# A gathered two-layer adapter with LayerNorm on one core: a new order of the first transfers, other runs of W1, two-part tables and later stores

## The reference

```python
w1 = W1[language_ids]                       # [512, 128] of ten
w2 = W2[language_ids]                       # [128, 512] of ten
h = relu(einsum('bsh,bha->bsa', hidden, w1) + b1[ids])
y = hidden + einsum('bsa,bah->bsh', h, w2) + b2[ids]
normed = (y - mean(y)) * rsqrt(var(y) + 1e-5)
out = x + normed * gamma[ids] + beta[ids]
```

## Time and profile before

| | us |
|---|---|
| median of 3 runs (316.99 to 318.69) | 318.01 |
| the profiled execution | 316.75 |
| its span | 315.0 |
| outside the span (316.75 - 315.0) | 1.75 |

### The profile page before, as it was taken

How to read it: one execution, slowest core, us unless ns; L and a number is a source line. 1 busy time by engine, 2 the same in 40 slices (tenths; PEclk the granted TensorE clock), 3 DMA queues, 4 the chain that set the end, 5 groups by cost and what they waited for, 6 DMA issues and landing times.

```text
span 315.0 us, 7506 instructions
## 1 busy us (share of the span) xinstructions
PE 289.5 (92%) x2008; PEld 253.8 (81%) x2039; DVE 289.8 (92%) x621; ACT 263.0 (83%) x601; POOL 186.2 (59%) x217
## 2 busy tenths in 40 slices
PE   1757959999999999999999999999999999999972
PEld 1237758889998888998888998888999888999861
DVE  5998856999999999999999999999999999999996
ACT  3977438889988889899989988999989988988872
POOL 2960742666655666565566665656656566665562
PEclk9968779999999999999999999999999999999998
DMA  5999999899999999899898989999898889885324
GB/s 155 332 389 372 293 331 390 276 340 352 358 347 328 321 313 302 302 318 318 292 315 313 299 309 310 318 302 311 290 319 311 315 304 311 286 291 202 116 110 177
DMA packets 56441, 94.03 MB, mean 298 GB/s; under 512 B 3387, under 2 KB 14711, under 8 KB 56273
## 3 DMA queue, kind: packets, MB, share of 16 engines
q1 hardware_dynamic: 56302, 93.41, 87.4%
q10 hardware_dynamic: 99, 0.14, 0.1%
HBM read 44.78 MB, written 33.55 MB: 249 GB/s over the span
## 4 chain that ended last, share of the span: by engine, by line
PE 79%; SPq 10%; issue 3%; DMA 3%; DVE 2%; DVEq 1%; ACT 0%
PE ps_h L504 33%; PE ps_y L525 28%; PE ps_T L488 16%; SPq L287 5%; DMA x_io<-in_x 2%; PE ps_h L497 2%; SPq L269 2%; SPq L257 1%; SPq L282 1%; DVE ps_y L663 1%; DVE ps_y L644 1%; SPq L172 1%; SPq L250 1%; DVEq L172 1%; DMA ids_raw<-in_itok_B 1%
## 5 line engine op out<-in xcount | busy, mean ns | idle before, releaser
L358 POOL TENSOR_TENSOR x_io<-x_io,beta_all 128x512 f32<-128x512 f32 x128 | 163.0, 1284 | 37.3 <-DVE ps_y L644 27.9
L504 PE MATMUL ps_h<-x_T,w_stage 128*128 128x128 f32 x1024 | 126.2, 277 | 0.0
L504 PEld LDWEIGHTS ps_h<-x_T,w_stage 128*128 128x128 f32 x1024 | 121.0, 194 | 0.8
L421 ACT ACTIVATE cut<-ps_y,row_sum 128x512 bf16<-128x512 f32 x128 | 87.9, 687 | 16.3 <-PE ps_y L525 11.4
L676 DVE SCALAR_TENSOR_TENSOR x_io<-ps_y,rstd,x_io 128x512 f32<-128x512 f32 x128 | 90.2, 747 | 2.6 <-DVE rstd L668 0.3
L663 DVE SCALAR_TENSOR_TENSOR ps_y<-ps_y,neg_mean,gamma_all 128x512 f32<-128x512 f32 x128 | 90.3, 750 | 1.7 <-ACT cut L421 1.7
L488 PE MATMUL ps_T<-identity,x_io 128*128 128x128 f32 x512 | 69.4, 280 | 11.2 <-DMA x_io<-in_x 10.1
L488 PEld LDWEIGHTS ps_T<-identity,x_io 128*128 128x128 f32 x512 | 62.2, 145 | 20.8 <-issue 12.6
L401 ACT COPY x_T<-ps_T 128x1024 f32<-128x1024 f32 x64 | 63.5, 992 | 6.7 <-PE ps_T L488 6.5
L525 PE MATMUL ps_y<-w_high,h_high 128*128 x128 | 62.3, 486 | 3.9 <-DVE w_low L625 2.2
L644 DVE SCALAR_TENSOR_TENSOR ps_y<-x_io,b_all 128x512 f32<-128x512 f32 x93 | 62.9, 704 | 0.0
(11 more groups left out here) (67 smaller groups left out, 150.9 us busy)
## 6 DMA issues: line engine op xcount, KB each, us to landing
x_io<-in_x SPq DMA_DIRECT2D x64, 512.0 KB, 5.1
out<-x_io SPq DMA_DIRECT2D x63, 512.0 KB, 3.9
w_stage<-w_all SPq DMA_DIRECT2D x58, 256.0 KB, 3.3
w_stage<-in_L_cond_W SPq DMA_DIRECT2D x12, 256.0 KB, 6.5
x_io<-in_L_cond_W SPq DMA_DIRECT2D x5, 512.0 KB, 7.8
b_all<-in_L_cond_b SPq DMA_DIRECT2D x1, 2560.0 KB, 14.3
w_all<-in_L_cond_W SPq DMA_DIRECT2D x5, 512.0 KB, 7.2
out<-x_io SPq DMA_DIRECT2D x2, 256.0 KB, 2.0
```

The source lines that it names most:

```text
L358: nc.gpsimd.tensor_tensor(x_slot(t), x_slot(t), of_lang(beta_all, lang), ALU.add).then_inc(x_beta_ready, 1)
L421: nc.scalar.activation(squares[:, t % 2, :], ps_y[t % Y_BANKS][:, :], ACT.Square, scale=-float(H), bias=stat(row_sum, t), accum_out=stat(s ...
L504: last = nc.tensor.matmul(bank[:, b * S:(b + 1) * S], w1_stage[:, 2 * (p % STAGE_PAIRS) + b, c, :], x_T[:, (2 * p + b) % 4, c, :], start=F ...
```

## The change

Seven things, none of which changes what is computed (gamma and beta are carried in two parts of float32r instead of three of bf16).

- SP's order: W2 chunks 0 and 1 ahead of the wait for the ids, then W1 of pair 0 and the other W2 chunks, then x and W1 of pairs 1 to 3 and x of pair 4; only then `b2_all`, and `w1_all` chunk by chunk between later loads.
- W1 of the first nine pairs comes from HBM, and a partition takes four neighbouring rows of it, one run of 2 KB instead of four of 512 B. So that the product is the same, the transposes of these nine pairs read every fourth column of x (`rows_of`).
- 24 slots of x. The store of a pair stands two turns later on SP, and a load waits for a store two turns old.
- gamma and beta are cut in two parts; TensorE's operand `signed_pick` (+1, -1) takes the difference. Their rows lie in `b2_all`, the parts in `w2_low`, until these are filled; hence four waits before `b2_all`.
- b1 is cut on GpSimd; b2 is centred on VectorE (`centre_b2`); the `pick` copy on ScalarE is gone.
- `put_b2` is gone: VectorE seeds the first four batches with x (`seed_x`), and TensorE adds b2 in S(0) and S(1).
- TensorE, ScalarE and VectorE take the beginning in another order; `copy_w1` is one step later.

```diff
-STAGE_HBM = 6
+STAGE_HBM = 9
+STORE_LAG = 2
@@ sync
+            load_x(0)
+            load_w2(0)
+            load_w2(1)
             sp.wait_ge(ids_ready, 1)
             stage_w1(0)
...
+            for p in range(1, 4):
+                load_x(p)
+                stage_w1(p)
+            load_x(4)
+            sp.wait_ge(b1_parts_ready, 1)
+            sp.wait_ge(b2_parts_ready, 1)
+            sp.wait_ge(beta_parts_ready, 1)
+            sp.wait_ge(gamma_parts_ready, 1)
             sp.dma_start(b2_all[:, :, :], b2.partition_broadcast(128)).then_inc(s_b2, 16)
...
-            for p in range(PAIRS - 1):
+            for p in range(PAIRS - 1 + STORE_LAG):
                 if p + STAGE_AHEAD < PAIRS:
                     stage_w1(p + STAGE_AHEAD)
-                sp.wait_ge(out_ready, 2 * p + 2)
-                sp.dma_start(out_pairs[:, p, :, :], x_pair_slots(p)).then_inc(stored[p % X_PAIRS], 16)
-                if p >= 1 and p - 1 + X_PAIRS < PAIRS:
-                    sp.wait_ge(stored[(p - 1) % X_PAIRS], x_loads(p - 1))
-                    load_x(p - 1 + X_PAIRS)
+                if p == 0:
+                    load_w1(4)
+                ahead = p + X_FIRST + 1
+                if ahead < X_PAIRS:
+                    load_x_behind_w2(ahead)
+                elif ahead < PAIRS:
+                    sp.wait_ge(stored[ahead % X_PAIRS], x_loads(ahead - X_PAIRS))
+                    load_x(ahead)
+                if p >= STORE_LAG:
+                    store(p - STORE_LAG)
@@ scalar
-            act.wait_ge(pick_step, 3)
-            nc.scalar.copy(pick[:, :, :], pick_row[:, :].unsqueeze(2).broadcast_to([128, L, 128])).then_inc(pick_ready, 1)
-            act.wait_ge(s_b2_rows, 16)
-            nc.scalar.activation(b2_cut[:, 1, :], b2_rows[:, :], ACT.Identity, accum_out=b2_sum[:, :])\
...
@@ tensor
+                rows_of = "s (p c) -> s c p" if t // 2 < STAGE_HBM else "s (c p) -> s c p"
+                columns = x_slot(t).rearrange(rows_of, c=C)
                 for c in range(C):
-                    last = nc.tensor.transpose(ps_T[:, t % 2, c, :], x_io[:, t % SLOTS, c * 128:(c + 1) * 128],
-                                               identity[:, :])
+                    last = nc.tensor.transpose(ps_T[:, t % 2, c, :], columns[:, c, :], identity[:, :])
...
-                table = parts[:, 0:H] if n < L else parts[:, H:2 * H]
-                nc.tensor.matmul(spread_bank(n), pick[:, n % L, :], table, start=True, stop=True).then_inc(spread, 1)
+                nc.tensor.matmul(spread_bank(n), signed_pick[:, n % L:n % L + 1].broadcast_to([128, 128]),
+                                 table_parts[:, n // L, :], start=True, stop=True).then_inc(spread, 1)
...
+            for p in range(FIRST):
+                first_half(p)
...
+            for p in range(FIRST, PAIRS):
+                n = p - FIRST
+                for b in range(2):
+                    second_product(2 * n + b, langs[n][b])
+                first_half(p)
```

More of the change, by code:

```diff
@@ L67, in build @@
         b2_all = sb("b2_all", [128, L, H], F32)
[L71 to L75, removed]
+        squares = sb("squares", [128, 2, H], BF16)
+        b2_parts = sb("b2_parts", [128, H], BF16)
+        table_parts = w2_low[:, L - 2:L, :]
+        rounded = b2_all[0:2 * L, 0:2, :].bitcast(F32R)
+        gamma_rows = b2_all[0:2 * L, 2, :]
+        beta_rows = b2_all[0:2 * L, 3, :]
+        b1_rows = b2_all[0:3 * L, 4, 0:A]
+        b2_rows = b2_all[0:3 * L, 5, :]
+        b2_cut = squares[0:3 * L, 0, :]
+        b1_cut = squares[0:3 * L, 1, 0:A]
         b1_parts = sb("b1_parts", [128, A], BF16)
@@ L187, in vector_seeds @@
             return t + 1 - scalar_seeds(t)
[L189 to L194, removed]
         def w1_stagings(q):
-            return sum(16 if scalar_copies(r) else 32 for r in range(q % STAGE_PAIRS, q + 1, STAGE_PAIRS))
+            return sum(32 if r < STAGE_HBM else 16 for r in range(q % STAGE_PAIRS, q + 1, STAGE_PAIRS))
         def wait_seed(engine, t):
@@ L266, in stage_w1, with load_w1 @@
                     sp.wait_ge(s_w1, 16 * W_CHUNKS)
-                table = w1_rows if q < STAGE_HBM else w1_all
-                for b in range(1 if scalar_copies(q) else 2):
+                table = w1_runs if q < STAGE_HBM else w1_all
+                for b in range(2 if q < STAGE_HBM else 1):
                     sp.dma_start(w1_stage[:, 2 * (q % STAGE_PAIRS) + b, :, :], table[:, bass.ds(langs[b], 1), :, :])\
                         .then_inc(w1_staged[q % STAGE_PAIRS], 16)
+            def load_w1(n):
+                langs = slice(n * LC, (n + 1) * LC)
+                sp.dma_start(w1_all[:, langs, :, :], w1_rows[:, langs, :, :]).then_inc(s_w1, 16)
@@ L272, in _, with load_x_behind_w2, store @@
+            def load_x_behind_w2(p):
+                sp.wait_ge(w2_low_ready, (p - X_FIRST + 1) * LC)
+                load_x(p)
+            def store(p):
+                sp.wait_ge(out_ready, 2 * p + 2)
+                sp.dma_start(out_pairs[:, p, :, :], x_pair_slots(p)).then_inc(stored[p % X_PAIRS], 16)
+            load_x(0)
+            load_w2(0)
+            load_w2(1)
             sp.wait_ge(ids_ready, 1)
             stage_w1(0)
-            load_w2(0)
-            load_w2(1)
-            load_x(1)
@@ L551, in _ @@
             pe.wait_ge(spread_dve, len(by_dve))
[L552 to L570, removed]
+            for p in range(FIRST):
+                first_half(p)
+            pe.wait_ge(ids_ready, 1)
+            langs = {p: langs_of(pe, p) for p in range(FIRST)}
+            pe.wait_ge(b2_parts_ready, 1)
+            pe.wait_ge(w2_low_ready, L)
+            for p in range(FIRST, PAIRS):
[3 more added lines that the diff above has]
+                first_half(p)
+                langs[p] = langs_of(pe, p)
             for n in range(PAIRS - FIRST, PAIRS):
@@ L585, in _ @@
             nc.vector.tensor_scalar(lang_ids[:, :], ids_fix[:, 1, :], 0.0, float(L - 1), ALU.max, ALU.min).then_inc(ids_ready, 1)
-            def cut_in_three(table, rounded, to, first, ready):
-                for k in range(2):
-                    nc.vector.tensor_copy(rounded, table).then_inc(cut_step, 1)
-                    dve.wait_ge(cut_step, first + 2 * k + 1)
-                    nc.vector.scalar_tensor_tensor(table, rounded, later_part[0:3 * L, k:k + 1], table,
-                                                   ALU.mult, ALU.subtract).then_inc(cut_step, 1)
-                    dve.wait_ge(cut_step, first + 2 * k + 2)
-                nc.vector.tensor_copy(to, table).then_inc(ready, 1)
             dve.wait_ge(pick_step, 3)
@@ L679, in _, with centre_b2 @@
             dve.wait_ge(neg_over_h_ready, 1)
-            for n in range(W2_AHEAD):
-                mean_of_w2(n)
+            def centre_b2():
+                dve.wait_ge(s_b2_rows, 16)
+                nc.vector.reduce_sum(b2_sum[:, :], b2_rows, axis=mybir.AxisListType.X).then_inc(b2_summed, 1)
+                dve.wait_ge(b2_summed, 1)
+                nc.vector.tensor_scalar(b2_neg_mean[:, :], b2_sum[:, :], -1.0 / H, None, ALU.mult).then_inc(b2_mean_ready, 1)
+                dve.wait_ge(b2_mean_ready, 1)
+                nc.vector.tensor_scalar(b2_rows, b2_rows, b2_neg_mean[:, 0:1], None, ALU.add)\
+                    .then_inc(b2_centred, 1)
+            mean_of_w2(0)
+            centre_b2()
+            mean_of_w2(1)
+            mean_of_w2(2)
             for n in by_dve:
```

144 lines of the change are left out of this document (77 added, 67 removed).

## The result

| | before | after |
|---|---|---|
| median, us | 318.35 (316.99 to 319.49, 4 runs) | 325.2 (324.29 to 330.94, 4 runs) |
| ratio | | 1.022 [1.016, 1.027] |
| a second series, us | 317.84 (315.86 to 319.5, 13 runs) | 327.34 (325.33 to 328.44, 4 runs) |
| ratio | | 1.032 [1.027, 1.036] |

The change makes the kernel slower; 311.0 was forecast, with 308.8 to 318.6 as range.

The account below looks back on a forecast made before the run. TensorE was taken as the bound, full from 60 to 270 us at 4.285 us a pair, so only an earlier start pays: F(4) 6.9 us earlier, other terms 0, said as 7.0; 318.01 - 7.0 = 311.0, range 308.8 to 318.6.

Parts of the forecast that it names:

- ScalarE's way to T(1): Beginning: b2 centring moves to VectorE, so ScalarE copies sooner; 1.4 of 1.6 us taken, T(1) at 20.05 instead of 21.45.
- From T(1) to S(0): Beginning: ScalarE's W2 rounding ends at 28.3, VectorE's last rest 0.7 later; S(0) at 29.2 against 32.21, gain 3.0.
- From S(0) to F(4): Beginning: 11.8 us of full-speed pieces plus 1.7 for slow clock, instead of 17.34; F(4) at 42.7, 6.9 us earlier.
- Transfers of the first fifty microseconds: DMA loads in the beginning: x of pairs 5 to 8 lands with 3 to 4 us slack; term 0.
- C: Rival: x of pairs 5 to 8 comes 3 to 4 us late, a 3.5 hole at T(7) or T(8); 314.5, chance 0.10.
- E: Rival: GpSimd or VectorE holds T(1) and S(0) at old times, only T(4)'s hole goes; 313.5, chance 0.13.
- The sign that the W1 loads from HBM land sooner than 6.5 us: W1 loads from HBM: expected to land sooner than the 6.5 us typical before.
- Transposes with every fourth column: T(0) to T(8) read x with a 16-byte step: price 0 to 1.07 a pair, 7.5 at most; 0 taken.
- B: Rival: strided loads at half speed, T 1.74 instead of 0.87, 7.0 us over eight pairs; 318, chance 0.20.
- D: Rival: each strided column served alone, T 3.48, 2.6 more on eight pairs; 332, chance 0.10.
- My sign "not 0.87": T(5) to T(8): the forecast is wrong if these are not 0.87 us on the chain.
- The rest: Middle and end: more W1 from HBM, fewer ScalarE copies, later store and the load behind it; 0 each.

Follow-up runs that it names:

- the other profile: The changed kernel, no edit: the profiled execution of its first series, which took 330.94 us.
- the paced kernel: Changed kernel with one more wait on SP: after the W1 copy, for pair p's output before the x load and store; 314.31 us, ratio 0.990.
- GpSimd's wait: The paced kernel with GpSimd's first beta addition held until the last rest of W2; 311.85 us, ratio 0.981.
- the burst: The changed kernel's SP row: W1 copy, x load, store issued back to back at F's end; 327.34 us. Put into the kernel before: 333.4 us.

## Why the prediction was wrong

- **ScalarE's way to T(1)**: right. 20.05 forecast, 20.02 measured (20.36 in the other profile).
- **From T(1) to S(0)**: 29.2 forecast, 30.36 measured (32.65 in the other profile, where the first sum of W2 started at 11.09 instead of 8.40). ScalarE's last rounding ended at 28.20, forecast 28.3. The term "VectorE's last rest takes 0.7 more" was mis-sized: two rests took 2.41 us here and 3.09 in the paced kernel, beside GpSimd's first beta additions (25.81 + 3.01 and 28.26 + 3.44), and 1.41 with these held back, when S(0) stood at 29.84. The Trainium skill (SBUF — State Buffer, "SBUF: two separate sides") has the rule: a VectorE instruction with two SBUF inputs and a GpSimd one that reads SBUF share a port pair as an exclusive lock. The rests have two, x staging and `w_high`, and the rows agree. The additions began at 31.41 before, in the middle of the last rests (30.66 + 1.41); the rests kept their 1.41, and the additions, which came second, took 3.02. The forecast never asked what GpSimd, begun earlier, runs beside.
- **From S(0) to F(4)**: 13.5 us forecast, 13.17 measured, right in this trace. It was 11.8 at the full clock and 1.7 for a slow one, and the second part is not always there: seven of the twelve profiles of the new beginning have 11.63 to 11.65 us, five have 12.5 to 13.6. F(4) at 42.7 was forecast, and 42.15 to 43.53 measured in five of nine profiles without GpSimd's wait (44.2 to 46.3 in the others). In four of the five S(0) came 1.3 to 1.9 us later than forecast and the way from there was 1.9 shorter, so that hit is in part luck.
- **Transfers of the first fifty microseconds**, rivals C and E: no wait for x, T(1) not held in this trace (19.8 to 21.4 in all twelve). The sign that the W1 loads from HBM land sooner than 6.5 us did not come: 7.0, with 18 of them.
- **Transposes with every fourth column**: nearly right for the sum, not for the reason. T is 0.95 on the chain instead of 0.87 for the strided pairs, T(8) the last:

```profile
55.98 0.95 PE ps_T L512 x8
...
60.23 0.87 PE ps_T L512 x8
```

  0.08 on eight pairs is 0.6 us; the prices of rivals B (0.87) and D (2.6) are refuted. My sign "not 0.87" came all the same. The load itself did become longer, by half (ns min/median/max, strided and from 60 us on):

```profile
L512 PEld LDWEIGHTS ps_T<-identity,x_io x41: 143/211/212, 38.1 to 59.8; 128*128 128x128 f32 x41
L512 PEld LDWEIGHTS ps_T<-identity,x_io x368: 138/140/143, 60.1 to 269.8; 128*128 128x128 f32 x184
```

  But the loads overlap: they start 135 ns apart instead of 127. So the rule of the Trainium skill that spoke against the change (SBUF — State Buffer, "Specifications", cachelines) is borne out in the load, 71 ns on 140, and shows in T at a tenth of the size I gave it. Undoing the stride together with the runs of W1 changed nothing that can be told.
- **The rest**: here the prediction failed. "The later store and the load behind it: loads come eight pairs ahead and TensorE does not wait for x in the middle today: 0". It was 14.5 us. I asked whether the transfers still come in time, not what they do to others when they start together, and no rival was about the middle. The earlier trace rows say only that TensorE was full, not by how much: behind it stood a read of 1.34 us in the median and 1.73 at most (90 to 270 us), in an instruction that isn't counted as busy, where 1.64 is what it may last. The median had 0.30 us to spare, the longest none. The read's median then rose to 1.97 us. Once that read is out of the way with everything else as changed, the time is 311.57, and the forecast's gain of 7.0 measures 6.6.

What stays open is why the read lengthens. That SP's new row does it is shown from both sides: put into the kernel before it brings the loss, and taken apart in the changed kernel it takes the loss away. That closeness alone is not enough is shown by the store ahead of the x load. Whether order or spacing is what counts, and by what path the transfers delay a read of eight bytes, was not measured.

## What to carry to other kernels

A wait that seems idle can be what spaces and orders transfers: before taking one out, list what is then issued in the same microsecond and in which order, and which engines read registers from memory then. Of a full engine ask for its margins: each instruction that is not counted as busy, its longest case, and the work that covers it. Of two profiles, ask whether the stretch ahead of the edit is the same before giving the whole difference to the edit. Where one engine's work moves earlier, look what it now runs beside, not only what it waits for.

## What the hardware showed that I had not expected

- A read of two ids lasted 0.53 us at least and 1.97 in the median in the burst, up to 2.11 (90 to 270 us); a read of four lasted 0.33 in the median and 0.71 at most in the same burst. Why is not known. Behind a long read TensorE's next matmul started 0.27 us after its end.
- The same three transfers, begun within the same 1.7 us, gave reads of 1.40 us in the median with the store ahead of the x load, and of 1.97 with the x load ahead.
- VectorE's and GpSimd's instructions on SBUF, side by side, took 3.09 for 1.41 us and 3.44 for 2.53.
- A transpose's weight load with a 16-byte step took 211 ns instead of 140, but eight transposes took only 0.08 us more, some 10 ns each.
